# TensorE's order inside a slot of an eight-head attention: value product first, scores last

## The reference, cut to what matters

```
q, k, v = (to_heads(q), to_heads(k), to_heads(v))
q = q * DH ** (-0.5)
sim = jnp.einsum('bhid,bhjd->bhij', q, k)
attn = jax.nn.softmax(sim, axis=-1)
out = jnp.einsum('bhij,bhjd->bhid', attn, v)
out = out.transpose(0, 2, 1, 3).reshape(b, -1, INNER)
return out @ Wo + bo
```

## Time and profile before

| | before |
|---|---|
| time, median of 3 runs | 1740.88 us (1731.67 to 1745.69) |
| profiled execution, span (no other time of it is given) | 1757.2 us |
| PE busy, DVE busy, ACT busy, POOL busy | 92%, 69%, 55%, 24% of the span |
| this attention, 1118.73 to 1467.78 us: PE busy | 333.46 of 349.05 us |
| the same: DVE busy, ACT busy | 272.12 and 225.13 us |
| transfers in that stretch | DMA share 0.00 |

### The profile page before, as it was taken

How to read it: one execution, slowest core, us unless ns; L and a number is a source line. 1 busy time by engine, 2 the same in 40 slices (tenths; PEclk the granted TensorE clock), 3 DMA queues, 4 the chain that set the end, 5 groups by cost and what they waited for, 6 DMA issues and landing times.

```text
span 1757.2 us, 24776 instructions
## 1 busy us (share of the span) xinstructions
PE 1625.3 (92%) x8448; PEld 1378.7 (78%) x8448; DVE 1213.5 (69%) x2336; ACT 962.8 (55%) x1845; POOL 426.6 (24%) x621
## 2 busy tenths in 40 slices
PE   4999979799899999799899987799999999999998
PEld 3898857589788887699778865688888888888886
DVE  4455579688666667557577765677777777777777
ACT  2343567355555555344687764566666656555554
POOL 6411231421321121410102113323232235012110
PEclk6576799799999999768999999899999999999999
DMA  5111133101010000101122100000000001121100
GB/s 154 33 28 37 37 85 121 32 23 55 1 37 19 19 28 10 37 19 55 41 69 96 46 15 0 1 1 1 1 1 1 1 1 53 33 85 53 56 25 24
DMA packets 28378, 63.01 MB, mean 36 GB/s; under 512 B 7499, under 2 KB 11519, under 8 KB 26207
## 3 DMA queue, kind: packets, MB, share of 16 engines
q1 hardware_dynamic: 28255, 61.45, 11.5%
HBM read 49.33 MB, written 1.25 MB: 29 GB/s over the span
## 4 chain that ended last, share of the span: by engine, by line
PE 79%; DVE 9%; POOL 5%; issue 3%; ACT 2%; SPq 1%; DMA 0%; ACTq 0%; DVEq 0%; POOLq 0%
PE psum L1383 14%; PE psum L1385 13%; PE psum L1384 13%; PE psum L1566 8%; PE psum L1698 5%; PE psum L1699 5%; PE psum L1700 5%; PE psum L1553 4%; PE psum L1799 3%; PE psum L1536 2%; PE psum L1538 2%; POOL rstd L620 1%; PE psum L1398 1%; POOL xn L640 1%; POOL xn L641 1%
## 5 line engine op out<-in xcount | busy, mean ns | idle before, releaser
L1238 DVE TENSOR_TENSOR hhl<-psum,hhl 128x512 fp32r<-128x512 f32 x464 | 317.9, 686 | 90.5 <-ACT hhl L871 88.2
L859 ACT ACTIVATE act_out<-psum 128x512 f32<-128x512 f32 x256 | 153.1, 598 | 247.4 <-PE psum L1385 246.9
L1383 PE MATMUL psum<-xh,wl 128*128 128x512 f32 x688 | 277.9, 404 | 9.2 <-DVE onorm L1149 4.9
L1234 DVE TENSOR_TENSOR psum<-act_out,psum 128x512 f32<-128x512 f32 x256 | 177.9, 695 | 149.4 <-PE psum L1385 141.3
L871 ACT ACTIVATE hhl<-psum 128x512 fp32r<-128x512 f32 x464 | 275.2, 593 | 1.9 <-DVE psum L1234 1.8
L1385 PE MATMUL psum<-xh,wh 128*128 128x512 f32 x688 | 273.0, 397 | 0.0
L1384 PE MATMUL psum<-xl,wh 128*128 128x512 f32 x688 | 272.8, 397 | 0.0
L1698 PE MATMUL psum<-hhl,wl 128*128 128x512 f32 x448 | 180.2, 402 | 11.0 <-DVE xn L1258 7.8
L1699 PE MATMUL psum<-hhl,wh 128*128 128x512 f32 x448 | 177.9, 397 | 0.0
L1700 PE MATMUL psum<-hhl,wh 128*128 128x512 f32 x448 | 177.2, 396 | 0.0
L861 ACT ACTIVATE psum<-psum 128x512 f32<-128x512 f32 x208 | 121.1, 582 | 74.6 <-PE psum L1385 73.3
(11 more groups left out here) (253 smaller groups left out, 3464.4 us busy)
## 6 DMA issues: line engine op xcount, KB each, us to landing
shared<-comb_dram SPq DMA_DIRECT2D x16, 1024.0 KB, 4.7
wraw<-in_f_dram SPq DMA_DIRECT2D x16, 768.0 KB, 5.1
shared<-comb_dram SPq DMA_DIRECT2D x32, 256.0 KB, 5.5
wraw<-in_f_dram SPq DMA_DIRECT2D x9, 512.0 KB, 5.2
hhl<-qh SPq DMA_DIRECT2D x64, 64.0 KB, 2.0
hhl<-ql SPq DMA_DIRECT2D x32, 64.0 KB, 2.0
wraw<-in_f_dram SPq DMA_DIRECT2D x8, 256.0 KB, 2.9
k<-qh SPq DMA_DIRECT2D x32, 64.0 KB, 2.0
```

Of the source, the lines that this page charges most:

```text
L859: ins = a.activation(act_out[k % 2][:], bank(f.g_banks[k % 2]), f.func)
L1234: v.tensor_tensor(h_bank(f, k), act_out[k % 2][:], h_bank(f, k), ALU.mult).then_inc(f.hf_done, 1)
L1238: v.tensor_tensor(hl[k % 4], h_bank(f, k), hh[k % 4].bitcast(f32), ALU.subtract).then_inc(f.h_ready, 1)
L1383: mm(dst, ll, rh, start=start, stop=False)
```

## The change

In TensorE's loop over the slots the value product of slot n, `wide_attend(n - ATTEND)`, moves from the end of the slot to its beginning, and the scores move from the beginning to behind the turn. The extra work now ends the slot. No instruction is added or removed, and no semaphore, count or buffer is changed; ACT, DVE, POOL and SP keep their lists.

```diff
                 for n in range(SLOTS + TURN):
-                    if score_tile(n) is not None:
-                        scores(score_tile(n))
+                    if n >= ATTEND:
+                        wide_attend(n - ATTEND)
                     if n == TURN:
                         pe.wait_ge(F2.y_used, F2.NS)
                     if n >= TURN:
                         turn(n - TURN)
+                    if score_tile(n) is not None:
+                        scores(score_tile(n))
                     for what, b in WPLAN.get(n, []):
...
-                    if n >= ATTEND:
-                        wide_attend(n - ATTEND)
```

## The result

The changed kernel took 1985.12 us (median of 4, 1953.0 to 1996.3) against 1741.22 us: ratio 1.131, 95% interval 1.120 to 1.143. Run again beside the last experiments it took 1959.09 us (1939.3 to 1967.0) against 1740.29: 1.123, 1.111 to 1.135. Forecast: 1945, range 1920 to 1990. Both medians lie inside; the first is 40 us above the number, the second 14.

The account below looks back on a forecast made before the run. TensorE bounds the stage and would wait for DVE's low half behind the row maximum. Slots +189.1, head +0.7, tail +7.0, logits +4.5, batch ends +3: +204 us on 1741 gives 1945, range 1920 to 1990.

Parts of the forecast that it names:

- The slot with scores: From one slot's last score matmul to the next slot's: row maximum, low half, value product, turn, scores, 3.69 us.
- The slot without scores: Slots with n % 5 = 4: no row maximum ahead of the low half, 2.01 us from turn to value product.
- the unit: Five slots, 3 x 3.69 + 6.50 = 17.57 us; the stage has 30 units and 3 slots, 538.2 us against 349.05.
- Row maximum ahead of the low half: In DVE's list the row maximum, needing this slot's scores, precedes the low half; TensorE idles about 1.5 us a slot.
- Rival 2: Only the turn's own chain counts, without queueing behind the row maximum: every slot 2.81 us, about 1829 us; 4%.
- Extra work is free: "v" and "q" products, 0.7 to 0.8 us each, stand inside TensorE's idle time and cost nothing after the change.
- Batch ends: Three times, the next batch's first value product waits for ACT's copy behind a late exponential: about 1.0 us each, +3.
- Logits: Three times, the "q" product waits for DVE's ranking: about 1.1 us, and 0.4 from the late row maximum; +4.5.
- The tail: From the last score matmul to the next stage's first product: 17.05 us against 10.03 before, +7.0.
- rival 1: The clock falls as well: about 2165 us if the whole stage runs low, 2000 if a quarter does; 8%.
- Rival 3: Extra products waiting for bank 7 no longer hold up value products: stage up to 11 us shorter, about 1730; 2%.
- Adding the sum to the median: The +204 us is added to the runs' median, 1741, not to the profiled execution's span of 1757.2 us.

Follow-up runs that it names:

- e6: Changed kernel with DVE's row maximum taken over 296 of the 589 keys; 1931 us, ratio 1.105.
- e7: Kernel before the change with the row maximum taken over 296 of the 589 keys; 1747 us, ratio 1.003.
- e1: Changed kernel with DVE's low half placed ahead of the row maximum in each slot; 1891 us, ratio 1.085.
- e10: Kernel before with only the value product moved to the slot's beginning, scores staying ahead of the turn; 1960.8 us, ratio 1.128.
- e8: Changed kernel with the slot's extra work moved ahead of the scores, between turn and scores; 2004.2 us, ratio 1.150.
- e11: Changed kernel with unread transposes added behind the extra work of every slot from 6 to the last; 1949 us, ratio 1.121.
- e9: Changed kernel with the value product two slots behind its turn, batch-end extra work kept in the slots of the kernel before; 1772.2 us, ratio 1.013.
- e3: Kernel before with only scores and turn changing places, the value product staying last in the slot; 1752.5 us, ratio 1.005.
- e2: Kernel before with DVE's low half placed ahead of the row maximum in each slot; 1873 us, ratio 1.072.

## Why the prediction was right, point by point

- **The slot with scores**, 3.69 us: 3.68, in its parts too (0.33, 0.69 from row maximum to low half, 0.74 to the value product, 0.80, 0.36, 0.76). I had 0.77 + 0.69 for DVE; the low half starts 0.08 earlier than the row maximum's recorded end, and the six score matmuls behind a turn take 0.07 longer, since the first is followed by the second after 0.21 us and not 0.14. Two errors of one size and opposite sign: that the sum is right to 0.01 us is luck, that it is right to 0.1 is not.
- **The slot without scores**, 2.01 from turn to value product: 2.01, and so the unit: 4 x 3.68 + 2.81 = 17.53 against 17.57. The stage, from the last score matmul of slot 5 (1136.35) to that of slot 158 (1691.27), took 554.9 us, inside the 540 to 560 given. The waits for low halves add up to 175.6 us and not 200, since an extra product fills part of some.
- **Row maximum ahead of the low half** as the reason: shown by e6 and e7, dose for dose, and by e1. Rival 2, 2.81 us a slot once the low half no longer queues, is what e1 built: 2.8 to 3.3 us, 1891 and not 1829, for a ring through ACT that I had not seen. So the sentence that the new wait is not that ACT and DVE need time was too strong: with the queueing gone 80 of the 219 us came back, and 139 stayed. And e10 says what I had not: with the value product this early, the row maximum isn't the only way to lose it; the order that keeps the row maximum early loses the scores as cover and lands at 3.63.
- **Extra work is free**: shown for "v" by e8. For "q", which stands in slots without scores, it is read from the rows above and was not tested by itself. The idle time before these products fell from 10.8 us to 5.8, of which 5.2 are the logits':

```profile
L1383 PE MATMUL psum<-xh,ab 128*128 128x512 f32 x30 | 14.8, 495 | 5.8 <-DVE logits L1023 5.2
```

- **Batch ends**, 1.0 us each: the wait was 2.36 and not 1.46, 0.9 more. **Logits**, 1.1 us: 1.72 us of idle time ahead of the "q" product, 0.79 from there to the value product, which comes at 1332.31 where 2.01 behind its turn would be 1331.20: 1.1. With all waits filled (e11) these slots show the same at the upper clock, 0.9 longer at each batch end and 1.45 at a logit wait, against 1.0 and 1.1 + 0.4.
- **The tail**, forecast 17.05 us from the last score matmul to the next stage's first product: 1691.27 to 1713.63, 22.4, because the last slots ran at the lower clock, 3.91 us each and not 2.81.
- **The term that was missing** is the clock. I put all of it into rival 1 with 8%, and took 1.00 for the forecast. It happened in part: 13 to 17 us in the stretch, 8 to 12 of them shown to be clock by e11, not the 55 or 219 of the rival. The ordinary rhythm keeps the upper level for up to 139 us at a time (1432 to 1571); most of the longer waits, the stage's beginning and its last slots lose it, and once, at 1674, the rhythm without extra work did. The Trainium skill, "TensorE: Matmul & The Clock Gate", section "A second HAM failure mode: psum-queue depth-cycling", says that short, frequent pauses can make the clock swing. This trace agrees in the last slots (0.50 at waits of 1.41 us) and not in the slots between (1.00 at 1.46 us). Rival 1 should have been a term of the sum for the long waits, and not an all or nothing case.
- **Rival 3**, bank 7 relieved: the waits did fall, by 5 us in a loss of 220, but since TensorE waits for DVE behind them anyway no run shows that this gave any time back.
- **Adding the sum to the median** was sound, but the spread that I took from three runs (±7) was too small: the code ahead of the change alone varies by 50 us between profiles. So it is in part luck that the first median, 1985, still lies in a range that ends at 1990; one of its four runs, 1996.3, doesn't. The stretch is the better test: 204 forecast, 217 and 221 measured.

## What to carry to other kernels

Before a consumer is moved forward in one engine's list, walk its operand's way through the other engines' lists and write down what stands ahead of each step there; a producer that waits for the mover's own last instruction turns two engines that overlapped into two that alternate. The cover of a chain is the distance, in work, between its start and its consumer: one more slot of distance gave most of it back (e9), and so did leaving the value product last (e3); with the value product first, neither order of scores and turn behind it did (e10). A swap on the helper engine can close another ring (e2), so price the whole cycle, row maximum, exponential, copy, low half, and not the one wait that one sees.

## What the runs showed of the hardware that I had not expected

- TensorE kept the upper clock with 2.24 us busy of 5 and pauses of 1.46 us. In the two profiles of this kernel it dropped to 1.2 GHz behind five of six waits of 2.36 us in that rhythm and behind three of six waits of 1.72 us for logits. The last slots, 2.8 us long with 1.4 us of wait and no scores, ran at that level in all five cases of the first profile and three of the second, and took 3.91.
- Unread work in the waits shortened the stretch: 566.1 against 574.2 and 578.6 us, at 3387 matmuls against 2110.
- The same code ahead of the change took 1083 to 1135 us in different executions, with granted clocks from 0.91 to 0.86 over it.
